# A graph attention layer's edge loop: message weights read straight from PSUM, and the banks of the attribute and node products regrouped

## The reference

```
h = (xn @ W.T).reshape(n, 8, 32)
alpha = sum(h[src]*a_src) + sum(h[dst]*a_dst) + sum(relu(edge_attr @ edge_W.T + edge_b) * h[dst])
alpha = leaky(alpha, 0.2)
ex    = exp(alpha - segment_max(alpha, dst)[dst])
out   = segment_sum(h[src] * ex / segment_sum(ex, dst)[dst], dst)     # edges are sorted by dst
```

## Time and profile before

| | |
|---|---|
| median of 3 runs | 4132.09 us |
| the profiled execution: time, span | 4141.2 us, 4139.4 us |
| mean granted TensorE clock | 0.942 |
| busy over the span: PE, DVE, ACT, POOL | 84%, 63%, 51%, 52% |
| share of the 16 DMA engines' time: POOL's queue, the two others | 26.1%, 9.7% and 5.4% |
| node tile loads (`hbt<-hsplit`) | 50 |

### The profile page before, as it was taken

How to read it: one execution, slowest core, us unless ns; L and a number is a source line. 1 busy time by engine, 2 the same in 40 slices (tenths; PEclk the granted TensorE clock), 3 DMA queues, 4 the chain that set the end, 5 groups by cost and what they waited for, 6 DMA issues and landing times.

```text
span 4139.4 us, 88906 instructions
## 1 busy us (share of the span) xinstructions
PE 3496.6 (84%) x22054; PEld 2355.6 (57%) x22055; DVE 2597.6 (63%) x6056; ACT 2103.2 (51%) x5703; POOL 2154.6 (52%) x2172
## 2 busy tenths in 40 slices
PE   4788899959988888889888988889889859909999
PEld 2447788835555555555554555555555548708888
DVE  5757655547877777777777777777777744401121
ACT  2312233326666666666666666666666634413232
POOL 3302000046777777777777777777777701061111
PEclk8999999979999999999999999999999989959999
DMA  4631011135555555555555555555555530021110
GB/s 150 201 124 48 28 32 34 35 93 127 138 138 138 141 139 140 141 139 142 141 140 137 138 143 142 143 141 143 143 145 146 141 120 28 21 63 36 35 39 25
DMA packets 352302, 449.27 MB, mean 109 GB/s; under 512 B 170970, under 2 KB 275163, under 8 KB 350456
## 3 DMA queue, kind: packets, MB, share of 16 engines
q0 software_dynamic: 95568, 267.78, 26.1%
q10 hardware_dynamic: 108050, 122.83, 9.7%
q1 hardware_dynamic: 148231, 53.53, 5.4%
HBM read 389.57 MB, written 55.13 MB: 107 GB/s over the span
## 4 chain that ended last, share of the span: by engine, by line
PE 60%; SPq 11%; DMA 10%; issue 9%; DVE 4%; ACT 2%; ACTq 2%; POOL 2%; POOLq 0%; DVEq 0%
PE bank L1099 13%; PE bank L1040 10%; SPq L420 5%; PE bank L1185 5%; PE bank L1197 5%; PE bank L1145 4%; PE bank L1005 4%; PE bank L1061 4%; PE bank L1014 4%; SPq L423 3%; DMA link<-links 3%; DMA al<-h_tab,idx 2%; PE bank L1030 2%; SPq L412 2%; PE bank L918 1%
## 5 line engine op out<-in xcount | busy, mean ns | idle before, releaser
L514 POOL DMA_INDIRECT al<-h_tab,idx x976 | 1056.4, 1082 | 302.6 <-issue 296.3
L514 POOL DMA_INDIRECT gbuf<-h_tab,idx x784 | 854.4, 1090 | 405.5 <-issue 392.2
L1040 PE MATMUL bank<-oneh_t,hbt 125*128 125x512 bf16 x2640 | 670.7, 392 | 147.9 <-DVE prod L1462 144.6
L752 ACT ACTIVATE enc<-bank,eb 128x512 f32<-128x512 f32 x880 | 552.9, 680 | 260.0 <-issue 177.5
L1462 DVE SCALAR_TENSOR_TENSOR prod<-enc,adst,bank 128x512 f32<-128x512 f32 x880 | 629.5, 737 | 32.8 <-PE bank L1040 31.2
L1099 PE MATMUL bank<-msg,oneh 128*125 128x264 f32 x2352 | 610.4, 404 | 15.3 <-DVE r L1551 7.0
L770 ACT ACTIVATE dist<-iota_n,dtile 128x125 f32<-128x125 f32 x1760 | 551.1, 384 | 1.6
L1040 PEld LDWEIGHTS bank<-oneh_t,hbt 125*128 x2640 | 235.3, 99 | 468.1 <-issue 276.2
L1099 PEld LDWEIGHTS bank<-msg,oneh 128*125 128x125 f32 x2352 | 429.7, 193 | 112.1 <-issue 43.3
L1061 PE MATMUL bank<-prod,hsel 128*32 128x128 f32 x7040 | 293.9, 286 | 123.2 <-issue 122.9
L1061 PEld LDWEIGHTS bank<-prod,hsel 128*32 128x32 f32 x7040 | 173.9, 111 | 323.3 <-issue 322.6
(11 more groups left out here) (255 smaller groups left out, 5492.8 us busy)
## 6 DMA issues: line engine op xcount, KB each, us to landing
dstb<-dst ACTq DMA_DIRECT2D x440, 125.0 KB
al<-pen_d SPq DMA_DIRECT2D x1760, 4.0 KB
att<-attrx ACTq DMA_DIRECT2D x880, 24.0 KB
al<-h_tab,idx POOLq DMA_INDIRECT x976
link<-links SPq DMA_DIRECT2D x880, 0.2 KB
gbuf<-h_tab,idx POOLq DMA_INDIRECT x784
attrx<-al ACTq DMA_DIRECT2D x8, 1176.0 KB, 12.3
hsplit<-hb POOLq DMA_DIRECT2D x25, 375.0 KB, 5.9
```

Of the source, the lines that this page charges most:

```text
L514: pool.indirect_dma_start(slot(n)[:, c, :], None, h_tab, bass.IndirectOffsetOnAxis(ap=idx[g % 2][:, k:k + 1], axis=0)).then_inc(gathered[n ...
L752: m = act.activation(enc[n % 2][:, k, :], bank[4 * (n % 2) + k][:, :], ACT.Relu, bias=eb[:, k:k + 1])
L1040: m = pe.matmul(bank[2 + k][:, :], hbt[:, ds(t & (HT - 1), 1), a, k * 128:(k + 1) * 128].rearrange("p t c -> p (t c)"), oneh_t[q][:, :], s ...
```

## The change

Four things change in the edge loop:

1. The weights of a group are turned (`g_turn`) into bank 4 or 5, by turns of the group, with a fresh start of the bank, and `m_msg` reads them there. ACT no longer copies them (`ex4` and L790 go); the small copy of the maxima stays, and `top_kept` takes the place of `ex_kept`. `g_turn` waits until the messages of the group two earlier are made.
2. The attribute products, which had banks 0, 1 and 4, 5 by turns, have banks 0 and 1 alone: `e_enc(n)` waits for `e_relu(n-1)`, where it had waited for `e_relu(n-2)`.
3. `d_ready` and `prod_ready` count halves: the first half of `e_dst(n)` waits only for the first half of `e_prod(n-1)`, and the first half of `e_prod(n)` only for the first half of `e_dst(n)`.
4. All waits on these two semaphores are rescaled to halves.

```diff
@@ -49,6 +49,7 @@
 NM = 3
 CLEARS = 10
 NDT = 4
+NDH = 2
 RING = 16
 RING_B = 7
 NGS = 6
@@ -258,7 +259,6 @@
         xs, exr = small[0], small[3]
         fmax, smax = al[:, spare + 128:spare + 256], al[:, spare + 288:spare + 416]
         ends = [al[:, spare + 255 + a:spare + 288 + a] for a in range(2)]
-        ex4 = small[4:6]
         top = sb("top", [1, H], at=mem_e)
         dl = sb("dl", [1, 2, H], at=mem_e)
         fac = sb("fac", [P, H], at=mem_e)
@@ -331,8 +331,8 @@
         enc_mm, prod_ready, r_ready, zeroed = sem("enc_mm"), sem("prod_ready"), sem("r_ready"), sem("zeroed")
 
         links_in = sems("links_in")
-        x_kept, x_local, ends_up, ends_read, links_made, ends_down, carry_read, x_dif, x_exp, ex_turned, ex_kept = (
-            sem("x_kept"), sem("x_local"), sem("ends_up"), sem("ends_read"), sem("links_made"), sem("ends_down"), sem("carry_read"), sem("x_dif"), sem("x_exp"), sem("ex_turned"), sem("ex_kept"))
+        x_kept, x_local, ends_up, ends_read, links_made, ends_down, carry_read, x_dif, x_exp, ex_turned, top_kept = (
+            sem("x_kept"), sem("x_local"), sem("ends_up"), sem("ends_read"), sem("links_made"), sem("ends_down"), sem("carry_read"), sem("x_dif"), sem("x_exp"), sem("ex_turned"), sem("top_kept"))
         dl_ready, fac_ready, acc_scaled = sem("dl_ready"), sem("fac_ready"), sem("acc_scaled")
         dt_ready, msg_ready, oneh_ready, dist_ready, acc_added, m_used = sem("dt_ready"), sem("msg_ready"), sem("oneh_ready"), sem("dist_ready"), sem("acc_added"), sem("m_used")
 
@@ -747,9 +747,9 @@
 
             def e_relu(n):
                 act.wait_ge(enc_mm, n + 1)
-                wait(act, prod_ready, n - 1)
+                wait(act, prod_ready, 2 * (n - 1))
                 for k in range(KC):
-                    m = act.activation(enc[n % 2][:, k, :], bank[4 * (n % 2) + k][:, :], ACT.Relu, bias=eb[:, k:k + 1])
+                    m = act.activation(enc[n % 2][:, k, :], bank[k][:, :], ACT.Relu, bias=eb[:, k:k + 1])
                 m.then_inc(enc_ready, 1)
 
             def keep_asrc(n):
@@ -784,10 +784,8 @@
 
             def g_keep(g):
                 act.wait_ge(ex_turned, g + 1)
-                wait(act, msg_ready, G * (g - 1))
                 wait(act, dl_ready, g)
-                act.activation(top[:, :], bank[7][0:1, B1:B1 + H], ACT.Copy)
-                act.activation(ex4[g % 2][:, :], bank[7][:, A1:A1 + 128], ACT.Copy).then_inc(ex_kept, 1)
+                act.activation(top[:, :], bank[7][0:1, B1:B1 + H], ACT.Copy).then_inc(top_kept, 1)
 
             def g_fac(g):
                 act.wait_ge(ends_down, g + 2)
@@ -823,7 +821,7 @@
                     g_keep(g)
                 if 0 < k < ITEMS - EB + 1:
                     b = k % EB
-                    act.wait_ge(d_ready, k)
+                    act.wait_ge(d_ready, 2 * k)
                     load_item((b - 1) % EB, s_next[b])
                     next_tile(t_next[b + 1], t_next[b])
                 if 0 <= k - 1 < ITEMS:
@@ -1025,20 +1023,21 @@
             def e_enc(n):
                 b = n % EB
                 pe.wait_ge(item_in[b // 2], 96 * (n // EB) + 96)
-                wait(pe, enc_ready, n - 1)
+                wait(pe, enc_ready, n)
                 for k in range(KC):
-                    m = pe.matmul(bank[4 * (n % 2) + k][:, :], ew_bf[32 * k:32 * k + 24, k * 128:(k + 1) * 128], att[b][32 * k:32 * k + 24, :], start=True, stop=True)
+                    m = pe.matmul(bank[k][:, :], ew_bf[32 * k:32 * k + 24, k * 128:(k + 1) * 128], att[b][32 * k:32 * k + 24, :], start=True, stop=True)
                 m.then_inc(enc_mm, 1)
 
             def e_dst(n, t):
                 q = n % 2
                 pe.wait_ge(oneh_t_ready, n + 1)
                 pe.wait_ge(node_in, t * 16 + 16)
-                wait(pe, prod_ready, n)
                 for k in range(KC):
+                    half = 2 * n + k
+                    wait(pe, prod_ready, half - NDH + 1)
                     for a in range(3):
-                        m = pe.matmul(bank[2 + k][:, :], hbt[:, ds(t & (HT - 1), 1), a, k * 128:(k + 1) * 128].rearrange("p t c -> p (t c)"), oneh_t[q][:, :], start=(a == 0), stop=(a == 2))
-                m.then_inc(d_ready, 1)
+                        m = pe.matmul(bank[2 + half % NDH][:, :], hbt[:, ds(t & (HT - 1), 1), a, k * 128:(k + 1) * 128].rearrange("p t c -> p (t c)"), oneh_t[q][:, :], start=(a == 0), stop=(a == 2))
+                    m.then_inc(d_ready, 1)
 
             def bank7_read(k):
 
@@ -1050,12 +1049,12 @@
                 if k % G == 2:
                     wait(pe, x_kept, min((k - 6) // G, NG - 1) + 1)
                 if k % G == 3:
-                    wait(pe, ex_kept, min((k - 11) // G, NG - 1) + 1)
+                    wait(pe, top_kept, min((k - 11) // G, NG - 1) + 1)
 
             def e_sum(n):
 
                 i = n % G
-                pe.wait_ge(prod_ready, n + 1)
+                pe.wait_ge(prod_ready, 2 * n + 2)
                 for k in range(KC):
                     for c in range(4):
                         m = pe.matmul(bank[7][32 * c:32 * c + 32, 0:128], hsel[:, i, :], prod[n % 2][:, k, c * 128:(c + 1) * 128], start=(i == 0 and k == 0), stop=False, skip_group_check=True)
@@ -1089,7 +1088,8 @@
 
                 pe.wait_ge(x_exp, g + 1)
                 pe.matmul(bank[7][0:1, B1:B1 + H], smax[:, 0:1], ident[:, 0:H], start=False, stop=False, skip_group_check=True)
-                pe.matmul(bank[7][:, A1:A1 + 128], exr[:, :], ident[:, :], start=False, stop=False, skip_group_check=True).then_inc(ex_turned, 1)
+                wait(pe, msg_ready, G * (g - 1))
+                pe.matmul(bank[4 + g % 2][:, 0:128], exr[:, :], ident[:, :], start=True, stop=True).then_inc(ex_turned, 1)
 
             def m_sum(n):
                 pe.wait_ge(msg_ready, n + 1)
@@ -1449,19 +1449,17 @@
 
                 b = n % EB
                 v.wait_ge(item_in[b // 2], 96 * (n // EB) + 96)
-                wait(v, d_ready, n - 1)
+                wait(v, d_ready, 2 * (n - 1))
                 v.tensor_scalar(oneh_t[n % 2][:, :], dstb[b][:, :], nid[0:P, ds(t, 1)], None, ALU.is_equal).then_inc(oneh_t_ready, 1)
 
             def e_prod(n, k):
 
                 q = n % 2
+                v.wait_ge(d_ready, 2 * n + k + 1)
                 if k == 0:
-                    v.wait_ge(d_ready, n + 1)
                     v.wait_ge(enc_ready, n + 1)
                     wait(v, r_ready, n - 1)
-                m = v.scalar_tensor_tensor(prod[q][:, k, :], enc[q][:, k, :], adst[:, k:k + 1], bank[2 + k][:, :], ALU.add, ALU.mult)
-                if k == KC - 1:
-                    m.then_inc(prod_ready, 1)
+                v.scalar_tensor_tensor(prod[q][:, k, :], enc[q][:, k, :], adst[:, k:k + 1], bank[2 + (2 * n + k) % NDH][:, :], ALU.add, ALU.mult).then_inc(prod_ready, 1)
 
             def mark(m):
 
@@ -1517,7 +1515,7 @@
 
             def g_delta(g):
 
-                v.wait_ge(ex_kept, g + 1)
+                v.wait_ge(top_kept, g + 1)
                 return mark(v.tensor_tensor(dl[0:1, 0, :], fin[0:1, 0:H], top[:, :], ALU.subtract))
 
             def g_delta2(g, known):
@@ -1535,10 +1533,10 @@
 
             def m_msg(n):
                 g, i = n // G, n % G
-                v.wait_ge(ex_kept, g + 1)
+                v.wait_ge(ex_turned, g + 1)
                 v.wait_ge(gathered[n % NGS], 64 * (n // NGS) + 64)
                 wait(v, m_used, n - NM + 1)
-                w = ex4[g % 2][:, :].rearrange("p (c i h) -> p c i h", c=4, i=G)[:, :, i, :]
+                w = bank[4 + g % 2][:, 0:128].rearrange("p (c i h) -> p c i h", c=4, i=G)[:, :, i, :]
                 v.tensor_tensor(msg[n % NM][:, :, :].rearrange("p c (h e) -> p c h e", h=H), slot(n)[:, :, 8:HR].rearrange("p c (h e) -> p c h e", h=H),
                                 w.unsqueeze(3).to_broadcast([128, 4, H, D + 1]), ALU.mult).then_inc(msg_ready, 1)
 ```

## The result

The changed kernel takes 3979.28 us (median of 4 runs, 3971.77 to 3984.97), the kernel before 4134.89 us beside it (4 runs, 4129.69 to 4149.17). The ratio is 0.9617 with a 95% interval of 0.9588 to 0.9647: 156 us less, where 147 were forecast. The profiled execution has a span of 3983.1 us and a mean clock of 0.953 (before: 4139.4 and 0.942).

What follows compares the result with a forecast made beforehand. POOL's gathers, stretched by the message product, were taken to bound the edge loop. Link stalls -157, tile loads +26 and direct edits -16 us gave 147 us saved: 3985 us against the median, range 3950 to 4080.

Steps and rivals of the forecast that it cites:

- The bound: Edge loop: POOL's gathers, without a pause and stretched by the message product, set the pace at 1.39 us a gather.
- The message product: DVE's product with weights read from PSUM: still 1.25 us, and expected to hold no gather.
- One item ahead: PE's attribute products: `e_enc(k+1)` now waits for `e_relu(k)`; cost 0, margin 1.05 us in the tightest step.
- Halves and the copy: Halves at the turn's step on PE: gain 0.1 us a group; ACT's dropped weight copy: 0.05 us a group.
- The bound of 0.24 us for added waits: Waits that halves add on PE and DVE: at most 0.12 us on each of two items between `fac` and turn.
- The loop without the gather limit: Edge loop paced next by ACT, its register loads and load issues: 20.75 - 0.05 - 0.1 + 0.24 = 20.84 us a group.
- the tile loads: About 50 node tile changes, each a 0.69 us load on ACT's queue, in three steps of four on ACT's chain: 26 us.
- The sum: Whole edge loop: 106 groups go from 22.23 to 20.84 us each, 147 us saved.
- Nothing changes: Rival: gathers stay stretched by something other than the second SBUF input, POOL keeps 22.2 us a group; 4115 to 4135 us; 10 in 100.
- Consumers slower: Rival: port is free, but PE's closer following of ACT and halves' waits give 21.6 us a group, 4065 us; 10 in 100.
- Half rate: Rival: broadcast PSUM operand read at half rate, message product 2.35 us, 4262 us; with milder forms 6 in 100.
- More than forecast: Rival: loop without stalls takes 20.4 us a group where ACT has slack; 194 us saved, 3938 us; 6 in 100.

## Why the prediction was right

**The bound.** POOL's gathers set the pace, stretched by the message product. Right: a gather takes 0.955 us for 1.087, and undoing the edit brings the longer ones back. One thing was not tried, the undoing beside a kernel before of 4130 us, so the step from 0.13 us a gather to 156 us in the time rests on the two traces: POOL ran without a pause at 22.2 us a group, which is above the 20.8 measured now; the link waits (46 times, 97 us) are gone; and POOL is held for the first time.

**The message product.** Forecast 1.25 us, measured 1.247. The rule of the Trainium skill on PSUM sources ("VectorE: DVE Perf Modes", TRN2 errata) doesn't show: 1247 ns for 1250. The rule of the Trainium skill on the shared port ("SBUF — State Buffer", "Who interferes with whom") holds both ways, for products with two SBUF inputs and with one. Its inference that a `tensor_tensor` spares descriptor generation is not settled by these gathers: they also read their indices from SBUF, and no run tells which of the two was held. What is shown is that an indirect gather as a whole is. The scans keep two SBUF inputs, and the forecast that they still hold a gather now and then is right: 33 of 1689 take over 1.1 us, at most 1.20.

**One item ahead.** Forecast no cost by a margin of 1 us. Measured 1.8 us in all. Right.

**Halves and the copy.** Forecast 0.1 and 0.05 us a group. No run separates them beside a kernel before of 4130 us, but the traces bound them together. Among groups without a tile load, a link wait or a lower clock, one took 20.71 us before and takes 20.46 now: 0.25, where 0.15 was forecast. PE's wait of 0.30 us for the node product is gone in full, so I probably gave away too much of it at `fac`. The bound of 0.24 us for added waits has no row behind it, and none shows. On the slower chips the halves are worth 0.6 to 0.9: the size depends on who else is late.

**The loop without the gather limit.** Forecast 20.84 us a group, measured 20.8, by the count of products and from turn to turn (104 groups, 20.76). Its terms: a group without a tile load was forecast at 20.60 and takes 20.49 (55 groups); the tile loads were forecast at 26 us in all and cost some 29 (49 groups of 21.08). The size of this second term is right partly by luck, for it comes about in another way than I gave, by the clock, which did not stay at 1.00. In order of time, changed kernel, a group with a tile load; below it the clock ahead of, in and behind the dip (busy time of each engine, then granted clock, DMA share, GB/s):

```profile
1353.80 2.02 PE L1099 MATMUL bank<-msg,oneh 128*125 128x264 f32 x8
...
1358.06 0.49 PE L1092 MATMUL bank<-ident,al 128*128 128x128 f32 x2
...
1364.20 0.29 ACTq L740 DMA_DIRECT2D hbt<-hsplit  x1
...
1373.63 0.16 ACT L794 ACTIVATE fac<-bank 125x8 f32<-125x8 f32 x1
...
1373.88 1.08 PE L1060 MATMUL bank<-prod,hsel 128*32 128x128 f32 x16 [1.94 <-issue]
...
1375.49 2.73 PE L1099 MATMUL bank<-msg,oneh 128*125 128x264 f32 x8
...
1380.46 0.49 PE L1092 MATMUL bank<-ident,al 128*128 128x128 f32 x2
...
1364.00:1373.00 9.00, 7.87 (x50) 4.32 (x48) 7.64 (x17) 5.11 (x15) 6.64 (x7) 1.00 0.67 174
1373.80:1377.80 4.00, 3.92 (x25) 3.14 (x26) 3.66 (x6) 1.97 (x6) 2.77 (x3) 0.59 0.44 113
1380.00:1384.00 4.00, 4.00 (x35) 2.62 (x32) 2.94 (x7) 2.53 (x9) 2.85 (x4) 1.00 0.53 137
```

The tile load at 1364.20 stands on ACT's queue ahead of `fac` (1373.63); `fac` is late, PE is idle for 1.94 us, and the granted clock of the 4 us behind it is 0.59, near the lower of its two levels (1.2 GHz, a clock of 0.50), with 1.00 on either side. The 16 sum products take 1.08 us instead of 0.65 and the 8 of L1099 2.73 instead of 2.02. From turn to turn this group has 22.40 us. I had put all dips to the link stalls, but eleven remain behind such waits, ten of them in groups with a tile load, with 22.2 to 23.2 us each; and before, ten of the 34 groups with a dip had no link wait. PE's longest idle time in the eleven is 1.5 to 2.4 us; 26 other groups have as much as 1.5 us or more and no dip. Without a dip a tile load costs 0.21 us (20.67 for 20.46), with one about 2 us. That the tile load is what makes `fac` late is read from the order of the rows and from the mean wait for `fac`, 1.31 us in groups with one and 1.01 without; no run leaves the loads out.

**The sum.** 156 us measured for 147. By groups from turn to turn: before, the 46 with a link wait took 23.7 us and the 60 others 21.1; now all take 20.76. So 46 x 2.6 = 120 us went with the link waits and 106 x 0.34 = 36 us besides. The forecast put 157 on the link stalls, with +26 for tile loads and -16 for the edits. It took the whole difference between the late and the early stretch for link stalls, though the late stretch had dips without them as well; the three terms come out right together and less so one by one.

**The rivals.** "Nothing changes" would have needed gathers at 1.09. "Consumers slower" would have shown in L1028 or L1039, which wait 1.8 and 0.3 us in all. "Half rate" fell with 1247 ns. "More than forecast" asked for 20.4 us a group in the whole loop; only the early stretch has it. Of the signs that the prediction named, two were missed by a little: the clock (0.99 for 1.00) and the wait for `fac`, 1.15 us a time for 1.2 to 1.6.

## What to carry to other kernels

Where POOL issues gathers without a pause, compare the duration of a gather that starts inside a long DVE instruction with one that doesn't. If it ends at a fixed time behind the DVE instruction (0.82 us here), whenever it began, move one of this instruction's two SBUF inputs to PSUM, even if its own time stays the same. And before sizing the gain, count the groups in a stretch where the bound engine still has a lead: that rate was the next limit here, within 1%. Count enough groups for it: over eight, one product more or less is already 0.3 us a group.

## What the runs showed of the hardware

- An indirect gather on POOL (128 rows, indices in SBUF) takes 0.95 us, with 0.30 us between two. Begun in the first 1.1 us of a 1.25 us DVE product with two SBUF inputs it ends 0.82 us behind that product; begun inside one with an input in PSUM it takes 0.945 us.
- The message product takes 1.25 us with its weights in SBUF and 1.25 us with them in PSUM.
- On four of the five chips of the study PE's semaphore updates come late, by a median of some 4 us for the turn, in both kernels, and the kernel before takes 4824 to 4875 us instead of 4130. The reading by chip matters: the change is worth 3.8% on one kind and 0.7% on the other, where it was measured on one chip. On the other kind undoing the weights costs nothing, while undoing the halves, forecast at 0.1 us a group, costs 1.6 to 2.0%.
